# One program for the projection, router, experts and last norm of a gated-delta and mixture-of-experts layer

## What is computed

```python
x = layernorm(x + gated_delta_attention(x) @ Wo.T)        # per token, over 256 values
scores = softmax(x @ gate_w.T)                            # 64 experts
idx = top_k(scores + gate_b, 6)                           # 6 experts per token
# each expert takes its first 128 tokens in order of token; others are dropped
h = silu(xb @ w1[e].T) * (xb @ w3[e].T)                   # per expert, inner size 176
y[token] += score * (h @ w2[e].T)
z = (silu(x @ ws1.T) * (x @ ws3.T)) @ ws2.T               # shared expert, inner size 352
x = layernorm(x + y + z)
```

## Time and profile before

| | us |
|---|---|
| median of 3 runs | 1820.45 (1818.24 to 1823.89) |
| the profiled execution, whole | 1832.13 |
| its span, first to last instruction | 1830.3 |
| PE / POOL / DVE / ACT busy in the span | 1620.1 / 870.2 / 1194.0 / 909.9 |

### The profile page before, as it was taken

One profiled execution on the slowest core, in us unless ns is written; L12 is line 12 of the kernel. 1 busy time (PEld: TensorE's weight loads), 2 busy tenths in 40 slices (PEclk: granted clock), 3 DMA queues, 4 the chain that ended last, 5 costly groups with the idle time before them and its releaser, 6 DMA issues. The chain is left out here.

```text
span 1830.3 us, 74010 instructions
## 1 busy us (share of the span) xinstructions
PE 1620.1 (89%) x31244; PEld 1240.8 (68%) x31244; DVE 1194.0 (65%) x3029; ACT 909.9 (50%) x2314; POOL 870.2 (48%) x1133
## 2 busy tenths in 40 slices
PE   6479999999999999999999999767999996688980
PEld 6235766676676677666766766756888886687870
DVE  1278888888888888888888888513555554122224
ACT  1266666666666666666666666411222221232333
POOL 0034343443444443443443443312777777567774
PEclk9799999999999999999999999878999998799995
DMA  6235555556556556455556455325555551599657
GB/s 272 81 74 123 115 114 122 123 113 125 118 117 124 121 113 132 110 120 125 118 115 133 104 116 127 72 62 186 156 175 154 174 155 57 147 246 250 109 87 281
DMA packets 521002, 245.45 MB, mean 134 GB/s; under 512 B 423504, under 2 KB 485584, under 8 KB 519776
## 3 DMA queue, kind: packets, MB, share of 16 engines
q1 hardware_dynamic: 368608, 200.75, 41.6%
q10 hardware_dynamic: 133632, 20.98, 6.2%
q0 software_dynamic: 18432, 18.99, 5.9%
HBM read 169.29 MB, written 71.37 MB: 131 GB/s over the span
## 5 line engine op out<-in xcount | busy, mean ns | idle before, releaser
L375 PE MATMUL delta_p_j<-delta_xt,delta_w 128*128 128x512 f32 x768 | 386.3, 626 | 31.3 <-DMA delta_xt<-in_xt 18.0
L575 DVE SCALAR_TENSOR_TENSOR delta_kq<-delta_hist,cw,delta_kq 128x512 f32<-128x512 f32 x384 | 295.5, 769 | 31.3 <-ACT delta_kq L723 24.2
L716 ACT ACTIVATE delta_hist<-delta_p_j 128x512 f32<-128x512 f32 x192 | 114.7, 598 | 253.0 <-PE delta_p_j L375 249.2
L889 POOL TENSOR_TENSOR delta_sd<-state,eg_end 128x256 f32<-128x256 f32 x128 | 104.2, 814 | 284.2 <-DVE state L655 284.2
L375 PEld LDWEIGHTS delta_p_j<-delta_xt,delta_w 128*128 128x128 f32 x768 | 131.6, 191 | 146.4 <-issue 111.7
L1248 POOL DMA_INDIRECT slot_tokens<-mix_tokens,mix_slot x192 | 189.6, 988 | 62.5 <-issue 61.9
L436 PEld LDWEIGHTS delta_p_i<-delta_kkq,rt 64*64 64x64 f32 x4096 | 129.7, 135 | 75.3 <-DVE delta_kkq L639 72.0
L864 POOL TENSOR_SCALAR delta_n<-delta_n 128x8 f32<-128x8 f32 x64 | 15.4, 241 | 298.7 <-DVE delta_n L606 298.7
L436 PE MATMUL delta_p_i<-delta_kkq,rt 64*64 64x32 f32 (+1 forms) x4096 | 142.8, 214 | 16.0 <-DVE delta_kkq L639 15.2
L1371 DVE SCALAR_TENSOR_TENSOR expert_gate<-expert_gate,expert_p_h 88x256 f32<-88x256 f32 x64 | 26.7, 418 | 178.8 <-ACT expert_gate L1391 178.8
L1342 PE MATMUL expert_p_h<-expert_xbt,w 128*88 128x128 f32 x1024 | 127.8, 279 | 14.4 <-ACT expert_xbt L1385 13.9
(11 more groups left out here) (145 smaller groups left out, 3652.4 us busy)
## 6 DMA issues: line engine op xcount, KB each, us to landing
delta_xd<-x_scratch SPq DMA_DIRECT2D x256, 128.0 KB, 4.2
delta_w<-in_wqkv SPq DMA_DIRECT2D x64, 416.0 KB
w<-in_w SPq DMA_DIRECT2D x64, 352.0 KB
delta_eg<-eg_rows SPq DMA_DIRECT2D x128, 130.0 KB
n_scratch<-delta_kkq ACTq DMA_DIRECT2D x128, 128.0 KB
mix_ot<-ot SPq DMA_DIRECT2D x16, 1024.0 KB
w<-in_w SPq DMA_DIRECT2D x64, 176.0 KB
ot<-delta_o SPq DMA_DIRECT2D x32, 256.0 KB
```

The source lines that it names most:

```text
L375: mm = pe.matmul(p_j[:, :], w[e][:, (ch * 3 + n) * 128:(ch * 3 + n) * 128 + 128], xt[m // 8 % 2][:, ch * 512:ch * 512 + 512], start=ch == ...
L575: ve.scalar_tensor_tensor(out, view(hist[e], i * 2 * 518 + tap, (259, 2), (1, 256)), cw[:, column:column + 1], out, ALU.mult, ALU.add).the ...
L716: ac.activation(view(hist[e], n * 518 + 3, (259, 2), (1, 256)), p_j[:, :], ACT.Copy)
L889: po.tensor_tensor(view(sd, 0, (128, 2), (C, 2), (1, C)), view(state, first_pair(group) * 128, (C, 2), (128, 2), (1, C)), view(s.eg_end, g ...
```

## The change

The three blocks become one, `ffn_phase`, with no barrier between them.

- `deviations(pair)` takes the place of `deviation(i)`: two GpSimd instructions for two tiles (128x2), in odd slots; the shift is gone. `mv` and `rstd` have two buffers for pairs.
- `normalise` is on VectorE, as `(y1 - mean) * rstd`, first in its slot, two tiles behind `residual`.
- All after it moves back: `turn(t-2)`, `route`, `top` and `choose` of `t-3`, `place`, `count_before` and `scatter` of `t-4`, `count_rest(t-5)`. The shared expert is four tiles behind the router (`LAG = 4`): `shared_up(t-7)`, `shared_down(t-8)`. There are 41 slots in place of 35. `x1` has 8 buffers, `x1t` 6, `y1` 4.
- GpSimd waits for its scatters, and loads the slot numbers through its own queue into `places`. SyncE waits for the adds and loads the groups. Experts and last norm reuse the buffers of the tiles and of `w13`.
- `s.ahead` is 25: 39 experts' weights are loaded after the tiles.

```diff
-        x1 = some(4, "x1", D + E)
+        LAG, PAIR = 4, 2
+        NX, NXT, NY = LAG + 4, LAG + 2, 4
...
-                if is_tile(t - 1):
-                    store_x1(t - 1)
-                if is_tile(t - 2):
-                    store_xz(t - 2)
+                if is_tile(t - 3):
+                    store_x1(t - 3)
+                if is_tile(t - 4 - LAG):
+                    store_xz(t - 4 - LAG)
...
+            for e in range(s.ahead, E):
+                sp.wait_ge(edown, e - s.ahead + 1)
+                expert_weights(sp, a, s, e)
             for i in range(2):
-                sp.wait_ge(xz_stored[i], 16 * NTILE // 2)
+                sp.wait_ge(added[i], 16 * E // 2)
+            for g in range(GROUPS):
+                sp.dma_start(total[g], rows(s.acc[0], g, 1)).then_inc(loaded[g], 16)
+                sp.dma_start(res[g], rows(s.acc[1], g, 1)).then_inc(loaded[g], 16)
...
+            def normalise(i):
+                pair, at = i // PAIR, i % PAIR
+                ve.wait_ge(power, pair + 1)
+                if i >= NX:
+                    ve.wait_ge(x1_stored[i % NX], 16 * (i // NX))
+                    ve.wait_ge(xz_out, i - NX + 1)
+                ve.tensor_scalar(x1[i % NX][:, 0:D], y1[i % NY][:, :], mv[pair % 2][:, at * 2:at * 2 + 1], rstd[pair % 2][:, at:at + 1],
+                                 ALU.subtract, ALU.mult).then_inc(x1_out, 1)
...
-            def deviation(i):
-                po.wait_ge(mv_out, i + 1)
-                if i >= 1:
-                    po.wait_ge(x1_out, i)
-                po.tensor_scalar(rstd[:, :], mv[:, 1:2], EPS, None, ALU.add).then_inc(eps, 1)
-                po.wait_ge(eps, i + 1)
-                po.tensor_tensor(rstd[:, :], rstd[:, :], s.minus_half[:, :], ALU.pow).then_inc(power, 1)
-                po.wait_ge(power, i + 1)
-                po.tensor_scalar(shift[:, :], mv[:, 0:1], rstd[:, 0:1], -1.0, ALU.mult, ALU.mult).then_inc(shifted, 1)
+            def deviations(pair):
+                po.wait_ge(mv_out, PAIR * (pair + 1))
+                if pair >= 2:
+                    po.wait_ge(x1_out, PAIR * (pair - 1))
+                po.tensor_scalar(rstd[pair % 2][:, :], view(mv[pair % 2], 1, (2, PAIR)), EPS, None, ALU.add).then_inc(eps, 1)
+                po.wait_ge(eps, pair + 1)
+                po.tensor_tensor(rstd[pair % 2][:, :], rstd[pair % 2][:, :], view(s.minus_half, 0, (0, PAIR)), ALU.pow).then_inc(power, 1)
...
+                if is_tile(t) and t % PAIR == PAIR - 1:
+                    deviations(t // PAIR)
+                if is_tile(t - 4):
+                    scatter(t - 4)
...
+                if e == 0:
+                    for i in range(2):
+                        po.wait_ge(xz_stored[i], 16 * NTILE // 2)
...
+            for i in range(2):
+                po.wait_ge(scattered[i], 16 * K * NTILE // 2)
+            po.dma_start(places[:, :], bass.AP(s.tok, 0, [[E, CAP], [1, E]])).then_inc(places_in, 16)
+            for i in range(NX):
+                po.wait_ge(x1_stored[i], 16 * NTILE // NX)
+            po.wait_ge(places_in, 16)
...
-        s.ahead = 28
+        s.ahead = 25
...
-        mix_phase(nc, a, s)
-        expert_phase(nc, a, s)
-        combine_phase(nc, a, s, out)
+        ffn_phase(nc, a, s, out)
```

More of the change, by code:

```diff
@@ L1105, in _ @@
+            turn_rows(0)
+            for t in range(E + 1):
+                if is_expert(t):
+                    hidden(t)
+                if is_expert(t + 1):
+                    turn_rows(t + 1)
+                if is_expert(t - 1):
+                    output(t - 1)
         @block.vector
```

404 lines of the change are left out of this document (178 added, 226 removed).

## The result

| | before | after |
|---|---|---|
| median, us | 1819.56 (4 runs, 1818.24 to 1823.89) | 1788.14 (4 runs, 1785.62 to 1791.49) |
| ratio | | 0.9824, 95% interval 0.9801 to 0.9848 |
| profiled execution | 1832.13, span 1830.3 | 1788.72, span 1786.9 |
| granted clock over the span | 0.956 | 0.966 |

The changed kernel is 31.4 us faster on this chip. The forecast was 1785.0. On two more occasions it came out the same way, and on one the other way: 2.6% slower than before. I call the places where the kernels ran the first to fourth chip. The second, third and fourth are different chips, each met once; for the first no chip number was kept, so it may be the same chip as one of the others.

A forecast was written before the change was run, and what follows sets the result against it. GpSimd's queue was taken to bound tiles and experts. Gains 25.8 + 0.9 + 5.6 + 4.1 less 0.9 make 35.5 us, so 1820.45 becomes 1785.0; own range 1779 to 1790, ends 1777 and 1798.

The forecast's parts named there:

- A paired deviation of 1.33 us, a pair of tiles in 16.6: GpSimd in the tiles: 14 paired deviations of 1.33 us replace 29 of 1.53, gain 25.8 us.
- First scatter 0.9 sooner: Start of the tiles: the first scatter moves to slot 4 but starts at 1267.2, 0.9 us sooner.
- Is GpSimd still never idle?: Tiles: TensorE's lead of 10 us or more loses 5.5 over 24 tiles, so GpSimd always has work queued.
- GpSimd waiting for `slot`: Sign in the tiles that the prediction would be wrong: GpSimd waits for slot numbers; no size given.
- rival 1: Tiles: TensorE and VectorE set the period, 9.6 us, and GpSimd starves 11 to 13 us: 1796 to 1798; chance 0.10.
- It hides: End of the tiles: TensorE's shared-expert work for four tiles, about four times 4.03 us, ends near the slot numbers' load.
- The norm on VectorE costs nothing: Tiles: one normalise of 0.2 to 0.5 us per tile on VectorE is covered; without cover, 12 us at most.
- the third rival: Tiles: the new normalise blocks GpSimd's scatters, up to 13 us lost: 1798, or 1792 at half; chance 0.13.
- Last scatter to first gather, 5.6: Between tiles and experts: GpSimd loads the slot numbers itself, landing to gather 3.3 us in place of 8.86, gain 5.6.
- Last add to last norm, 4.1: Between experts and last norm: SyncE waits for the adds' landing alone, gain 4.1 us (2 to 4.3).
- Three more experts' weights, -0.9: Experts: three more run beside weight loads, at 3.33 us in place of 3.03, so 0.9 us is lost.
- The fourth rival: Tiles: scatters' descriptors held up over 1.1 us per tile make the kernel slower, 1836 at 1.6 us; chance 0.03.

The follow-up runs named there:

- scatter3: The changed kernel with three scatters of slot numbers per tile in place of six, leaving out half the slot numbers; third chip, 1776.6 us, ratio 0.9749.
- lag2: The changed kernel with the shared expert two tiles behind the router in place of four, buffers as with four; fourth chip, 1783.7 us, ratio 0.9802.
- norm_act: The changed kernel with the norm of a tile back on ScalarE, its shift a small VectorE instruction per two tiles; third chip, 1785.0 us, ratio 0.9802.
- after_3: The changed kernel itself, run again on the third chip; 1785.7 us, ratio 0.9810.
- barriers: The changed kernel with the two barriers put back, at the end of the tiles and of the experts; second chip, 1871.5 us, ratio 1.0281.
- pair1: The changed kernel with deviations computed one tile at a time in place of two; second chip, 1852.6 us, ratio 1.0171.
- before_extra: The kernel before with one more small GpSimd instruction (128x1) per tile, on which nothing waits; second chip, 1824.7 us, ratio 1.0012.
- after_2: The changed kernel itself, run again on the second chip; 1870.4 us, ratio 1.0263.
- after_4: The changed kernel itself, run again on the fourth chip; 1787.7 us, ratio 0.9826.
- lag0: The changed kernel with the shared expert zero tiles behind the router in place of four, 37 slots; third chip, 1795.4 us, ratio 0.9849.
- after: The changed kernel itself in its first run and profile, on the first chip; 1788.14 us, ratio 0.9824.

## Why the prediction was right, and where it was not

In three of four comparisons the time was 1788.1, 1785.7 and 1787.7, for a forecast of 1785.0 and a range of 1777 to 1798.

- *What bounds the kernel: GpSimd's queue.* Right. `scatter3` gives its work back and the scatters end 22 us sooner.
- *A paired deviation of 1.33 us, a pair of tiles in 16.6.* Right: the power of two columns took 0.72 for 0.73, and a pair 16.52 for 16.6. The gain from first to last scatter was 27.0 and 24.2 for 25.8.
- *First scatter 0.9 sooner.* 0.9 and 1.8, with some luck: the first projection took 5.4 us for 6.6, the second 4.5 for 3.45, and the two misses cancel.
- *Is GpSimd still never idle?* No, by a small amount. It was right that TensorE is held back early, and wrong that its lead then lasts. The prediction named "GpSimd waiting for `slot`" as a sign of being wrong, and the sign came: 4.0 us of such waits in the tiles on the first chip, 8.5 and 8.3 on chips 3 and 4. The step left out that TensorE is held back in two pauses while its lead is built up (first by the power, then by `place`), and what the clock does after them. On the first chip the clock fell after the first pause, a projection took 1.7 us longer, and the ninth projection came 11.2 us before the tenth. On chips 3 and 4 it fell after the second; there these 11.2 us are 14.7 and 15.2. At 8.54 us per tile TensorE can't make that up, and GpSimd is at TensorE's pace from the middle of the tiles on. The last scatter came 2.0 and 2.5 us later after P0 than on the first chip. So rival 1 was right for the second half of the tiles, at a period of 8.54 in place of the 9.6 that it was priced with.
- *"It hides": the shared expert's last four tiles.* Right, by 4 us: TensorE ended at 1530.06 and then waited 3.98 us for the rows of the first gather (1531.02). `scatter3` and `lag2` show how near that was: with less of GpSimd's work it no longer hides, with two tiles of lag TensorE waits 13.4 us.
- *The norm on VectorE costs nothing.* 0.7 us by the medians of `norm_act` and `after_3`, which can't tell a few us from nothing. The row that I took for it, a scatter that had already started when VectorE did, was the harmless order. The other order is in the changed kernel behind 8 of 16 powers: 0.13 us each. So the third rival was right as a mechanism and off in size, about 1 us for 13, as far as the rows show it. The Trainium skill's "SBUF — State Buffer", section "SBUF: two separate sides", says that whichever of the two starts first holds the port until it ends. The order with VectorE first agrees with that: the row of normalise (0.41 us) and the scatter that began inside it (1.20 for 1.07). The other order agrees only in part: the instruction of 1403.59 ran its usual 0.26 us wholly inside a scatter that lasted to 1404.46, while some that began about the scatter's middle were stretched (last section).
- *Last scatter to first gather, 5.6.* 5.7 and 5.6, by rows alone. From the landing it took 3.1 us, for 3.3.
- *Last add to last norm, 4.1.* 4.1 and 4.2, by rows alone.
- *Three more experts' weights, -0.9.* Not there: first gather to last add was 1.3 and 2.1 us shorter. In 1650 to 1700 the transfer share was 0.71 with 31 gathers and adds, for 0.96 and 30 before.
- *The clock at the first experts, nothing.* The pause before them was 3.98 us and the clock still fell to 0.50, so it was nothing.
- *The sum, 35.5.* From P0 on the traces give 39.8 and 37.8, the medians of whole executions 31.4, 35.1 and on the third chip 36.7. That the forecast lies among them owes something to terms that missed in both ways: the experts' stretch gave 1.3 and 2.1 where 0.9 was to be lost, and the last scatter came 2.0 and 2.5 us later on chips 3 and 4 than on the first.

**The fourth rival and the second chip.** There the change was slower, which I had given 0.03, and through another mechanism than the one named. The rival said that GpSimd's descriptors would be held up; there they are the one thing that goes on, and TensorE, ScalarE, VectorE and SyncE are held up. No view of before on the first chip shows a trace of it, and no step of the prediction would have found it. (The rival's own price was off too: it said that a hold-up would have to be four times as long as the new instruction, but the 1.1 us that it starts from is under three times the measured 0.41.) Had the forecast been checked on that chip alone, it would have been wrong by 85 us.

What the runs say of its cause:

- It is not the missing barriers: `barriers` has them again and the same hold-ups.
- It is not the pairing: `pair1` has none, and the hold-ups stay, shorter and more often. Its scatters still come closer than before's (8.6 us per tile for 9.2), so their pace isn't ruled out.
- It is not only what the change brought: `before_extra` has one hold-up, in its last tiles, where a tile's scatters follow the last tile's after 7.8 us.
- It is not the transfers. In the tiles of `after_2` packets took as long as in those of `after_4` (instruction packets of 16 KB 1.03 us for 1.06 in the median, data packets 63 ns for 63 in the mean). The last instruction packet landed at 1282.9, as the hold-up shown above began, and the next only at 1319.3, well after its end. So late instructions, which I had suspected first, have no row for them.
- The records themselves differ on that chip, in all four kernels. Increments of semaphores recorded between 60 and 240 us after P0:

| | by engines | by transfers |
|---|---|---|
| chips 1, 3 and 4, nine traces with six scatters a tile | 655 to 684 | 3444 to 3764 |
| `scatter3` | 674 | 2680 |
| chip 2: `before_extra` | 345 | 1158 |
| chip 2: `after_2`, `barriers`, `pair1` | 385 to 390 | 718 to 787 |

In the attention, on the same chip, nothing is missing (3171 to 3203 by engines between 300 and 900 us of the span, for 3181 to 3201 elsewhere). It starts about with the first scatters. So on chip 2 about half of the engines' increments and more of the transfers' go unrecorded in the tiles, and about a quarter of the engines' in the experts' stretch (383 to 404 for 513 to 529). It is so in `before_extra` too, which has one hold-up and is 2.7 us over the kernel before, within the noise. The changed kernel makes slightly more of them (672 to 674 by engines and 3709 to 3741 by transfers elsewhere, for before's 655 to 661 and 3444 to 3478), and there everything that sends them stands still every third or fourth tile. Whether that small step makes the difference isn't shown. The Trainium skill says in "NOTIFIC — the notification-queue block", section "7.1 Overflow: three behaviours, one of which stalls the engine", that the block which writes such records can drop them where they leave it, and pushes back on what sends them when it is full inside. Missing records beside standing engines would fit a slow way out for them on that chip; no run here shows it. If it is so, the recording costs the time, and what this chip would take without it isn't known. That stays open, and so does whether it is the chip or the moment, since all four kernels ran there at one time and none again later. Open too is which part of the change makes them so frequent: the norm on VectorE and the shared expert's lag are what `pair1` and `barriers` share with the changed kernel, and `norm_act`, `lag0` and `lag2` met only chips without hold-ups.

## What to carry to other kernels

Where one engine's queue sets the pace, count its steps and gaps: the sum of rows gave each stretch within 3 us. But look at the second engine's floor as well; here it was 3% away, it was reached in the second half of the tiles, and the whole of what could still be had from the first queue was 9 to 13 us. Ask also where the second engine is held back while its lead is built up, for pauses there cost more than their length. And run a change on more than one chip before calling it a gain: the same program was 1.7 to 1.9% faster in three comparisons and 2.6% slower in one, with tight intervals on each.

## What the runs showed of the hardware that I had not expected

- A pause of TensorE of 2.8 us, in the middle of a busy stretch, was followed by the granted clock at 0.50 and a projection of 5.31 us in place of 3.62 in `after`, but in `after_3` and `after_4` the same pause was followed by a projection of 3.62; there the clock fell after the next one, of 2.2 and 2.8 us. The pause of 3.98 us before the first expert did the same to it (3.71 in place of 1.98).
- A small GpSimd instruction of 0.23 us put before a scatter cost 0.04 us each time: it lay in the issue gap.
- A scatter that starts while VectorE runs a single-source SBUF instruction takes 1.20 us in place of 1.07; one that has started before it keeps its 0.97, and then it can be VectorE that is stretched. In `after` the 128x64 instruction at L1237 took 0.25 us when it began up to 0.44 us after a scatter, and 0.30 to 0.51 when it began 0.48 to 0.73 us after; whatever its start, it ended about 1.0 us after the scatter's.
- A plain load issued from GpSimd's queue took 0.61 us to issue and 2.95 from its start to the first gather's; from ScalarE's queue the gather came 0.8 us sooner.
- On one chip of four, TensorE started matmuls without a wait between them 1.4 us apart, and increments reached ScalarE 10 to 16 us late, in a rhythm that two programs had in common to within 1 us. The kernel before with one small instruction more had one such hold-up there.
